# Transposes per token tile in stage A and fewer semaphore waits on TensorE in stage B of a pre-norm attention and feed-forward layer

## The reference

```python
h  = layernorm(x)                                   # no gain, no bias
qkv = einsum('btd,de->bte', h, Wqkv) + bqkv         # 1024 -> 3072
q, k, v = split(qkv, 3)
q = q / norm(q); k = k / norm(k)                    # over the width
kv = sum(k * v, axis=tokens)                        # one row of 1024 per sequence
x = x + einsum('btd,de->bte', q * kv, Wout) + bout

h = layernorm(layernorm(x))  with gain ln1_g, bias ln1_b
h = einsum('bsd,hd->bsh', h, ternary_quant(w1)) + b1    # 1024 -> 4096
h = gelu(h)
h = layer_norm(h, ln2_g, ln2_b)
x = x + einsum('bsh,dh->bsd', h, ternary_quant(w2)) + b2
```

## Time and profile before

| what | value |
|---|---|
| time, median of 2 runs | 2632.83 us (2627.07 to 2638.59) |
| the profiled execution | 2631.47 us |
| its span on the slowest core (7) | 2629.9 us |
| spans of the 8 cores | 2603.4 to 2629.9 us |
| granted TensorE clock, mean of core 7 | 0.824 |
| busy: PE, DVE, ACT, POOL | 63%, 38%, 29%, 4% |

### The profile page before, as it was taken

One profiled execution on the slowest core, in us unless ns is written; L12 is line 12 of the kernel. 1 busy time (PEld: TensorE's weight loads), 2 busy tenths in 40 slices (PEclk: granted clock), 3 DMA queues, 4 the chain that ended last, 5 costly groups with the idle time before them and its releaser, 6 DMA issues.

```text
span 2629.9 us, 35286 instructions; the slowest of 8 cores (2603.4 to 2629.9 us)
## 1 busy us (share of the span) xinstructions
PE 1647.2 (63%) x10928; PEld 912.4 (35%) x10928; DVE 1011.3 (38%) x2702; ACT 771.6 (29%) x1313; POOL 118.0 (4%) x217
## 2 busy tenths in 40 slices
PE   0155564454457235767867867867867867867867
PEld 0022222121123111534534534534534534534544
DVE  0556554444445223243243243243243243243243
ACT  0123346666564100322222222212212212212211
POOL 2101101111110000000000000000000000000000
PEclk9987777777678657878888888888888888888889
DMA  9855635554652580110010010010010010010000
GB/s 145 195 163 173 193 95 181 172 165 151 180 153 76 122 155 13 29 36 21 25 37 21 25 37 21 25 37 21 24 38 21 24 38 21 23 38 21 21 17 17
DMA packets 199497, 195.36 MB, mean 74 GB/s; under 512 B 156308, under 2 KB 156309, under 8 KB 199319
## 3 DMA queue, kind: packets, MB, share of 16 engines
q0 software_dynamic: 31200, 92.34, 13.0%
q1 hardware_dynamic: 153856, 67.17, 10.6%
q10 hardware_dynamic: 14264, 33.62, 3.4%
HBM read 117.55 MB, written 50.33 MB: 64 GB/s over the span
## 4 chain that ended last, share of the span: by engine, by line
PE 50%; DVE 12%; issue 9%; ACT 8%; DVEq 7%; DMA 7%; SPq 4%; POOL 1%; ACTq 1%; POOLq 0%
PE py L679 19%; PE py L720 17%; PE pqkv L580 7%; DMA wstg<-w 5%; PE patt L659 3%; DVEq L951 2%; DVEq L794 2%; SPq L316 2%; DVE outbuf L1035 2%; SPq L310 1%; DVEq L1042 1%; DVE kvtmp L835 1%; DVE xring L956 1%; ACT qhat L380 1%; ACT khat L389 1%
## 5 line engine op out<-in xcount | busy, mean ns | idle before, releaser
L580 PE MATMUL pqkv<-wqkvp,h1T 128*128 128x512 bf16 x1536 | 399.7, 427 | 380.2 <-DVE qkvb L824 327.5
L679 PE MATMUL py<-w2p,h4buf 128*128 128x512 bf16 x2048 | 556.3, 406 | 125.4 <-DVE outbuf L1043 124.0
L720 PE MATMUL py<-z1T,w1p 128*128 128x256 bf16 x4096 | 488.2, 284 | 166.6 <-ACT h4buf L487 164.9
L720 PEld LDWEIGHTS py<-z1T,w1p 128*128 128x128 bf16 x4096 | 386.4, 101 | 269.1 <-issue 171.5
L580 PEld LDWEIGHTS pqkv<-wqkvp,h1T 128*128 128x128 bf16 x1536 | 162.6, 108 | 616.5 <-issue 479.5
L993 DVE TENSOR_TENSOR h4sq<-h4buf 128x128 bf16<-128x128 bf16 x1024 | 223.3, 225 | 304.6 <-PE psumSQ L688 272.3
L487 ACT ACTIVATE h4buf<-py,beta1c 128x256 bf16<-128x256 f32 x512 | 241.1, 474 | 236.1 <-PE py L720 235.6
L1051 DVE CAST z1T<-pzT 128x128 bf16<-128x128 f32 x256 | 56.6, 284 | 568.1 <-PE pzT L700 567.5
L688 PE MATMUL psumSQ<-onesb,h4sq 128*128 128x1 bf16 x1024 | 167.5, 164 | 84.5 <-DVE h4sq L993 84.5
L688 PEld LDWEIGHTS psumSQ<-onesb,h4sq 128*128 128x128 bf16 x1024 | 104.3, 102 | 231.1 <-issue 125.9
L685 PE MATMUL psumSQ<-onesb,h4buf 128*128 128x1 bf16 x1024 | 174.6, 171 | 0.0
(11 more groups left out here) (125 smaller groups left out, 1272.6 us busy)
## 6 DMA issues: line engine op xcount, KB each, us to landing
wstg<-w POOLq DMA_DIRECT2D x128, 512.0 KB, 6.1
xbufA<-x SPq DMA_DIRECT2D x32, 512.0 KB, 5.2
xbufB<-x SPq DMA_DIRECT2D x32, 512.0 KB, 3.6
out<-outbuf ACTq DMA_DIRECT2D x32, 512.0 KB, 2.9
h1scr<-h1buf ACTq DMA_DIRECT2D x32, 256.0 KB, 5.2
qhscr<-qhat ACTq DMA_DIRECT2D x32, 256.0 KB, 2.3
wqkvp<-wqkv POOLq DMA_DIRECT2D x8, 768.0 KB, 27.1
wq1scr<-qod POOLq DMA_DIRECT2D x16, 256.0 KB, 3.2
```

What stands on the lines that cost most here:

```text
L580: mm = te.matmul(out=pq[i % 4][:, :], lhsT=h1T[:, (g % 2) * 4096 + c * 512 + s * 128: (g % 2) * 4096 + c * 512 + (s + 1) * 128], rhs=wqkvp ...
L679: mm = te.matmul(out=py2[:, hh * 512:(hh + 1) * 512], lhsT=h4m, rhs=w2p[:, m * D + hh * 512:m * D + (hh + 1) * 512], start=(m == 0), stop= ...
L720: mm = te.matmul(out=py1[m % 2][:, :], lhsT=w1p[:, c * H + m * 128:c * H + (m + 1) * 128], rhs=z1T[:, c * 256:(c + 1) * 256], start=(c == ...
```

## The change

It has three parts. In stage A, `h1t_tile(jt)` takes the place of `h1t_half(jt)`: eight transposes of 128 rows for one tile, which waits for the write of that tile alone, issued behind the x load of every tile from the third on. `ah1t` counts per tile, and PE waits on the handle of its tile. In `y2_tile` PE waits for `bh4` at every fourth step only, at the value that the fourth step from there would need. In the y1 pass PE waits for `bh4` at even m only, at 32p+m, the value that step m+1 needed before.

```diff
-            def h1t_half(jt):
+            def h1t_tile(jt):
                 gt = jt // 4
                 st = jt % 4
-                hg = jt // 2
-                sy.wait_ge(ah1w.h(0), 16 * (jt // 2 + 1))
-                sy.wait_ge(ah1w.h(1), 16 * (jt // 2 + 1))
-                if hg >= 4:
-                    sy.wait_ge(ah1t.h(hg % 4), 128 * (hg // 4))
+                sy.wait_ge(ah1w.h(jt % 2), 16 * (jt // 2 + 1))
+                if jt >= 4:
+                    sy.wait_ge(ah1t.h(jt % 4), 128 * (jt // 4))
                 if gt >= 2 and st == 0:
                     sy.wait_ge(aqkv.h, 24 * (gt - 1))
                 for c in range(8):
                     ah1t.inc(sy.dma_start(
                         out=h1T[:, (gt % 2) * 4096 + c * 512 + st * 128:
-                                (gt % 2) * 4096 + c * 512 + (st + 2) * 128],
-                        in_=h1_d[jt * 128:(jt + 2) * 128, c * 128:(c + 1) * 128],
-                        transpose=True), hg)
+                                (gt % 2) * 4096 + c * 512 + (st + 1) * 128],
+                        in_=h1_d[jt * 128:(jt + 1) * 128, c * 128:(c + 1) * 128],
+                        transpose=True), jt)
...
-                    if j >= 3 and j % 2 == 1:
-                        h1t_half(j - 3)
-            h1t_half(4 * NG - 2)
+                    if j - 2 >= 0:
+                        h1t_tile(j - 2)
+            for jt in (4 * NG - 2, 4 * NG - 1):
+                h1t_tile(jt)
...
-                    hg = 2 * g + s // 2
-                    te.wait_ge(ah1t.h(hg % 4), 128 * (hg // 4 + 1))
+                    te.wait_ge(ah1t.h(s), 128 * (g + 1))
...
                     q = 32 * j + m
-                    te.wait_ge(bh4.h, 32 * p + m + 1)
+                    if m % 4 == 0:
+                        te.wait_ge(bh4.h, min(32 * p + m + 4, 32 * (p + 1)))
...
                 for m in range(32):
-                    if 32 * p + m >= 2:
-                        te.wait_ge(bh4.h, 32 * p + m - 1)
+                    if m % 2 == 0 and 32 * p + m >= 2:
+                        te.wait_ge(bh4.h, 32 * p + m)
                     for c in range(8):
                         mm = te.matmul(
```

More of the change, by code:

```diff
@@ L1095, in build_program @@
     }
-    dexpect = {"ax": 16 * NT, "ah1w": 16 * NT, "ah1t": 64 * NT,
+    dexpect = {"ax": 16 * NT, "ah1w": 16 * NT, "ah1t": 512 * NG,
                "aqw": 16 * NT, "wld": 16 * NLOADS,
```

## The result

The changed kernel is slower. The ratio of its time to that of the kernel before, both run in turn on one chip, is 1.0636, with a 95% interval from 1.061 to 1.0663. On the 2627.5 us that the kernel before took there (median of 10) that is 2795 us, 167 us more. The plain median of its 12 runs is 2820.3 us. Executions in which the cores of one die were held at a lower clock are in that median but in no ratio and no median further down, and since the profiled execution (2891 us) is one of them, on cores 0 to 3, I read core 7 of both traces, which was not held back in either. The first view gives each core's span and mean granted clock.

A forecast was written before the change was run, and what follows sets the result against it. The prediction took PE's own work, 16 pairs of token tiles at 99 us each, to bound stage B; stage A was paced otherwise. Terms 195+6+13+0-15+0 = +199 us on 2632.8 gave 2832 us, range 2790 to 2885.

The forecast's parts named there:

- the class of 0.97: Whole kernel: chance 0.97 that the change makes it slower by over 2%.
- The stop: y1 pass: PE stops for a whole gelu round at even groups from m=4, 224 times 0.87 us, +195 us.
- The wait at m = 2: y1 pass, third group: the existing wait for ACT grows by 0.37 us, 16 times, +6 us.
- The clock after the long wait: y1 pass: half a pair of groups more at 1.2 GHz, 0.8 us a pass, +13 us.
- The clock in y2: y2: no clock term forecast; steps priced at 2.4 GHz and removed waits taken as 0.
- That bound of the range, -38: y2: gain of 38 us if the removed wait were all of a step's remaining 0.05 us.
- Stage A: -15 forecast: Start of stage A: split transposes let PE and DVE begin earlier, 15 us gained, ends 0 and 17.
- the gain stays: Stage A after its start: what follows is paced by its own chain, so the 15 us is kept.
- an upper end of +24: Steady part of stage A, forecast 0: half a load costs what a whole one does, +2 for a dozen tiles.
- rival 2: Stage A: the split makes SP or the DMA engines late, no gain at start and +24 after, 2871 us; chance 0.07.

The follow-up runs named there:

- e1: Kernel before with only the y1 wait changed (even groups wait for gelu m-1, odd groups for nothing); ratio 1.071, median 2828 us.
- e10: Kernel before with the late wait (gelu m-1) at every fourth y1 group only, seven stops a pass; 2732.4 us against its batch's 2630.3.
- e6: Kernel before with four y1 buffers (halves of py2 added), waits at even groups only, for gelus m-4 and m-3; ratio 0.9755.
- e2: Kernel before with only the y2 waits thinned, 8 instead of 32 a tile; ratio 1.0008.
- e9: Kernel before with the y1 and y2 waits changed, transposes as before; ratio 1.0581, median 2797.3 us.
- e7: Kernel before with the first half of the z1 transposes of tile j0+2 moved ahead of the attention product; ratio 0.9795, median 2588 us.
- e5: Kernel before with every y1 group waiting for the gelu of the group before it, 29 stops a pass; 3475.7 us, ratio 1.3163.

## Why the prediction was right, step by step

The forecast was +199 us and 2832, the result +167, 2795, in the range and in the class of 0.97. The mechanism was the right one, and the sizes of its terms can be checked one by one.

**The stop: right.** Forecast 0.87 us for each of 224, 240 waits of some 330 us, two groups in 2.62. Measured 2.62 for two groups and 331.0 us in 240. At 1.2 GHz I had 0.92; it is 0.87 there too (two groups of 1.71 and a stop take 1388.89-1384.61 = 4.28), because the 0.421 us that I used is the longest matmul (16 usual ones take 3.57 from first start to last end, which makes 0.37 for one). e1 shows that this edit is the whole loss, e10 that the cost goes with the number of stops, e6 that it is their lateness.

**The wait at m = 2: right.** +0.37 a pass, forecast and measured (12.78 to 13.15).

**The clock after the long wait: the wrong sign.** The step was "half a pair of groups more at 1.2 GHz, 0.8 us a pass, 13 us". The pass from the third group on grew by 11.62 us; fourteen stops of 0.87 are 12.2, so the clock gave 0.6 back, and the term is about -10. In most passes the low stretch lasts 10.2 us in both kernels and ends 17 us after the pass began; a stop now lies in it, so fewer matmuls do. Before, groups 2 and 3 and over half of group 4 ran cold, now 2 and 3. My error was to count in groups what goes by time. It isn't the whole story: in e1 and e10 the low stretch is often longer, and by the same account the clock cost 0.3 us a pass in e1 and 0.9 in e10, where I had forecast 0.8.

**The clock in y2: not in the sum at all, -22 us for the first tile and -4 for the second.** I had priced y2 by its steps at 2.4 GHz and put its waits at 0. e2 shows that to be right for the waits but for 0.2 us a pair; the y2 steps are 0.48 in all kernels. What went from the first tile is the stretch at 1406 to 1409, shown above: I had read the clock in the y1 pass only. The -4 of the second tile is not explained. The first steps of a pair gave 0.2 us, -3; e2 and e9 have that and e1 has not, so it is what the thinned waits of y2 are worth. Together it was -29 where the forecast had 0. That bound of the range, -38, was laid for cheaper steps of y2 and not for the clock, so that the result fell inside it was in part luck.

**Stage A: -15 forecast.** At its start the steps hold on core 7 (start us, length us):

```profile
96.05 11.95 SPq L282 DMA_TRANSPOSE h1T<-h1scr  x8
108.10 0.50 SPq L293 DMA_DIRECT2D xbufA<-x  x1
...
118.11 9.09 PE L578 MATMUL pqkv<-wqkvp,h1T 128*128 128x512 bf16 x32 [31.61 <-DMA h1T<-h1scr]
```

```profile
130.34 1.21 DVE L791 TENSOR_REDUCE stA<-xbufA 128x1 f32<-128x1024 f32 x1
...
133.10 2.48 DVE L823 TENSOR_TENSOR qkvb<-pqkv,bqkvb 128x512 f32<-128x512 f32 x4
...
140.29 0.69 DVE L823 TENSOR_TENSOR qkvb<-pqkv,bqkvb 128x512 f32<-128x512 f32 x1 [1.99 <-PE pqkv L578]
```

Transposes at 96 to 108 (forecast 99 to 113), first product at 118 (125 to 130), first drain at 133.1 (132.6), the sixth ended at 141.0 against the 155.1 of the earlier trace rows. But the mean of the 8 cores is 141.0 and 132.7 for the first drain, -8, and 854.6 and 849.4 for that of the last tile, -5. So the start was sized from core 7, which gained more there than the mean, and "the gain stays" was a step that failed. Over all traced kernels, by the mean of 8 cores, the five with split transposes start their drains at 134.2 and the eight others at 142.1, and they start those of the last tile at 850.6 and 853.3: of 8 us some 3 are left. Between the first drains of tiles 11 and 25 a tile takes 26.8 to 27.0 us with the split and 26.5 to 26.8 without it, some 0.4 more in the mean, about +5 where the forecast had 0 and an upper end of +24. The issues of SP cost what was said, and rival 2 did not come. The landings took 3.0 us for 128 rows; the 2.4 of the prediction was that of another tensor:

```profile
L282 SPq DMA_TRANSPOSE h1T<-h1scr x256: 1079/1202/2482, 96.0 to 830.7; - x128
...
DMA to landing us min/median/max: 2.2/3.0/13.0
```

The tiles now follow each other more evenly (28.4 and 27.3 us in these rows, where they took turns of 29.3 and 27.0), but not faster:

```profile
597.12 5.09 PE pqkv L578 x16
623.28 5.65 PE pqkv L578 x16
651.71 5.10 PE pqkv L578 x16
679.02 5.10 PE pqkv L578 x16
```

**The sum on core 7.** 199, less 22 in the pass (186 where 195+13 were forecast), less 29 in y2, and 3 more because stage A gave 12 there and not 15: 151, against 149 measured. The ratio gives 167. Most of the 16 between is the choice of core: core 7 was the slowest of the kernel before, 12 us above the mean of its eight cores (2617.9), and is an average one of the changed kernel, whose cores have a mean span of 2782.3 in the seven executions that the ratio uses, 164 more. Stage A is 7 of it, the 12 of core 7 against the 5 of the mean. The rest may be passes with a later rise: core 4 of the same execution has such, with 0.4 us more for the mean pass, a pair of 109.7 and a span of 2785.5, and the slowest core sets the time. The timed runs left no trace, so that stays open. So does what decides between a low stretch of 10 and of 17 us.

## What to carry to other kernels

A wait that is made rarer has to ask for the latest of the counts that it replaces. Before one is moved to every second group, write down which product that count belongs to, and whether its reader can have ended; with two buffers, waiting for the gelu of the group just issued takes away the second buffer at every wait. With the buffers to back it (e6), or where the awaited count was reached long ago (e2), the rarer wait is free. And read the clock through the whole repeating period before pricing a part of it: here edits of 0.2 to 1.6 us a pair changed how long PE ran at 1.2 GHz, in either direction, and that was worth as much as the edits themselves or more.

## What the runs showed of the hardware that I had not expected

- PE busy without a gap can be at 1.2 GHz: 3.00 of 3.00 us at 0.50 from 1406 on, 48 us after the pass began, behind holes of 1.14 and 0.61 us. The changed kernel has the same holes and stays at 1.00 there. e6 and e7, shorter by 3.4 and 2.5 us a pair, and the changed kernel, 10 us longer, don't have it on core 7.
- Holes of 0.72 us do not lower the clock once it is up: thirteen of them, one after each 1.91 us of matmuls, in a stretch of 60 us at 1.00. The same hole after every 1.86 us of matmuls at 1.2 GHz goes with a clock of 0.50 for 87 us on end (e5); with the hole after every 3.57 us at 1.2 GHz the clock was up again after one to three such rounds (changed kernel, e1).
- The mean granted clock is no measure of what a kernel loses by it. It was 0.847 in the changed kernel, 0.824 before, and 0.821 in the fastest one.
